# Value products one slot later, and one score product for both heads in narrow slots, in a fused attention and expert layer on one core

## The chip, the core and the metric

The kernel runs on one core of a Trainium2 chip. The metric is the device time in microseconds of one launch. TensorE does matrix products, VectorE and ScalarE read its result banks (PSUM), GpSimd works on SBUF only, and SyncE issues most transfers. Each engine works through its own list of instructions in order and waits on semaphores that the others raise.

## The reference

Batch 8, length 1024, width 256, 16 heads of 64, latent width 64, 32 experts:

```python
q = einsum('bld,dhk->blhk', x, Wq)
latent = einsum('bld,dc->blc', x, Wkv_down)
k = einsum('blc,chk->blhk', latent, Wk_up);  v = einsum('blc,chk->blhk', latent, Wv_up)
attn = softmax(where(causal, q k^T / sqrt(64), -inf))
x1 = layernorm(x + einsum('bqhd,hdo->bqo', attn v, Wout))
top1 = argmax(softmax(x1 @ w_router));  slot = expert's place if its place < capacity (320)
y = (silu(buf @ w_gate) * (buf @ w_up)) @ w_down        # per expert, on the gathered rows
out = layernorm(x1 + gate * y at the accepted tokens)
```

## The kernel before, in words

Wk_up is folded into the query weights and Wv_up into the output weights, so scores and value products are taken against the latent itself. The 16 heads are 8 pairs, the 8 batches give 64 pairs (`gp`; `b, p = divmod(gp, NPAIR)`). A pair is worked off in 12 slots (`SLOT`, line 48): slots 0 to 3 are the first 512 queries against key tiles 0 to 3, slots 4 to 11 the second 512 queries against key tiles 0 to 7. A tile on the diagonal needs only the queries from its own on, so slots 1, 2, 3 and 9, 10, 11 are 384, 256 and 128 queries wide for each head; slots 2, 3, 10 and 11 are the narrow ones.

For slot n (counted over all pairs), `turned_scores` (line 648) makes the scores with keys on the partitions, for each head two products: the high part of the latent (L660), then its low part with the row of negated maxima (L663). They go to `turned_ps[n % 2]`, a bank for each head. `exponentials` on ScalarE (L904) writes them into one of six buffers `probs`. `keep_past` on GpSimd (L440) zeroes the upper triangle of diagonal tiles, `add_probs` (L455 to L464) adds the buffer into the row sums. `values` on TensorE (L676) multiplies two slots' probabilities with the latent keys, both heads into `value_ps` (L683).

The maxima come from a second set of score products, `row_scores` (L636): two units in every slot, for the next pair, into the two banks `row_ps`. VectorE reduces each unit in turn (`row_max`, L1056 for diagonal units, L1060 for others), and unit n may start only once unit n - 2 is reduced. `turn_max` (L646) transposes eight columns of maxima, VectorE copies them (L1071) and SyncE puts them into `q_max` (L342 and L345).

All other products share one bank, `misc_ps`, in an order fixed by the tables `EARLY` and `LATE` (lines 240 to 280): in slot t of pair gp, TensorE does the scores, the `EARLY` uses, two units of row scores, the values, then the `LATE` uses. These are queries of the next pairs (`q`, L584), transposed maxima (`maxT`), row totals (`sums`, L693, turned and inverted by VectorE, L1077 to L1089), the output projection of the batch before (`proj`, L702, eight of them), its transposes (`x1T`, L720), router logits (L728) and counts of the places (`pos`, L736 to L741), and for the next batch the transposes of x (`xT`, L594), latents and keys. Each use waits until the reader of the one before has freed the bank. The other engines follow the same tables. Around them stand, at fixed pairs and slots, the steps of the layer norm and the routing: `variance` and `normalise` on VectorE, `roots` on GpSimd (L478 to L490), `choose` (from L1144) and `place` (from L1162) on VectorE, `gate_exponentials` on ScalarE, and GpSimd's `send` of rows to their experts' slots (L497), in pairs 4 and 5.

Before, the values of slots t - 2 and t - 1 come in every even slot t:

```python
if t % 2 == 0 and gp + t:
    values(gp * NSLOT + t - 2)
```

After the 64 pairs come `ENDING` (the last batch's rest) and then the 32 experts, which the change leaves as they are.

## Time and profile before

| | |
|---|---|
| time, median of 3 runs | 2686.41 us (2686.27 to 2687.94) |
| the profiled execution's own time | 2683.09 us |
| its span, first to last instruction | 2681.3 us |
| granted TensorE clock, mean | 0.972 of full speed |
| TensorE products busy | 2494.3 us (93%) |
| TensorE weight loads busy (beside products) | 1588.2 us |
| VectorE busy | 1550.2 us (58%) |
| ScalarE busy | 1002.2 us (37%) |
| GpSimd busy | 1701.7 us (63%) |

The spans are of one execution. PE is TensorE's product side, PEld its weight loads, DVE VectorE, ACT ScalarE, POOL GpSimd. A busy time is the union of its instructions' spans; matmuls overlap, and their ends are modelled. In a timeline, a row that merges several instructions gives the start of the first and the time to the end of the last; in brackets stands the idle time ahead of it and what ended it.

### The profile page before, as it was taken

Reading aid. Unit: us, or ns where it says so; the run is one execution under the profiler, and the core shown is the slowest. Engines: PE = TensorE matmul, PEld = TensorE weight load, DVE = VectorE, ACT = ScalarE, POOL = GpSimd, SP = SyncE. Lnnn points to the kernel's source line nnn. Section 1 sums busy time; section 2 is a strip of 40 time slices with the busy share of each in tenths; the row PEclk is TensorE's granted clock in tenths of the full one; section 3 lists DMA queues with packets and bytes.
Section 4 is the critical chain, followed back from the end, with each engine's and each line's share of the span. In section 5 each row is a group of like instructions: output and inputs, shape, how many; then the busy total and the mean of one; then the engine's idle time right before and its main releaser. Section 6 shows DMA issues by size and latency. Waiting matters only on the chain.

```text
span 2681.3 us, 35897 instructions
## 1 busy us (share of the span) xinstructions
PE 2494.3 (93%) x12072; PEld 1588.2 (59%) x12072; DVE 1550.2 (58%) x4378; ACT 1002.2 (37%) x1496; POOL 1701.7 (63%) x1671
## 2 busy tenths in 40 slices
PE   6999999999999999999999999999999999869996
PEld 4555665556655665566556655566556655646663
DVE  4566556665666566655665566656665665235553
ACT  3344334442444334433444244424443344112222
POOL 1677656865687658766786568656876578414444
PEclk7999999999999999999999999999999999879998
DMA  2121100200020001100110002000200011135441
GB/s 81 56 80 56 37 13 13 68 17 13 17 63 18 13 13 41 43 13 17 27 53 17 9 17 67 17 13 17 60 21 13 13 40 43 44 105 161 153 155 57
DMA packets 97062, 118.91 MB, mean 44 GB/s; under 512 B 12480, under 2 KB 75976, under 8 KB 96880
## 3 DMA queue, kind: packets, MB, share of 16 engines
q1 hardware_dynamic: 89712, 99.98, 13.3%
q0 software_dynamic: 7168, 16.64, 1.7%
q8 instruction: 98, 1.61, 0.2%
q14 instruction: 84, 0.69, 0.1%
HBM read 46.91 MB, written 37.90 MB: 32 GB/s over the span
## 4 chain that ended last, share of the span: by engine, by line
PE 63%; POOL 17%; issue 11%; DVE 5%; ACT 2%; DMA 0%; POOLq 0%; SPq 0%; ACTq 0%; DVEq 0%
PE value_ps L683 14%; POOL sums L464 10%; PE turned_ps L660 8%; PE row_ps L636 7%; PE turned_ps L663 7%; PE misc_ps L584 6%; PE turned_ps L844 5%; PE misc_ps L702 4%; PE misc_ps L693 4%; POOL probs L440 2%; PE value_ps L857 2%; PE misc_ps L857 2%; ACT probs L904 1%; POOL slots_x L497 1%; DVE masked_row L1056 1%
## 5 line engine op out<-in xcount | busy, mean ns | idle before, releaser
L904 ACT ACTIVATE probs<-turned_ps 128x1024 f32<-128x1024 f32 (+3 forms) x768 | 616.8, 811 | 959.6 <-PE turned_ps L663 951.3
L464 POOL TENSOR_TENSOR sums<-sums,probs 128x1024 f32<-128x1024 f32 (+3 forms) x512 | 830.2, 1622 | 23.2 <-ACT probs L904 14.2
L1056 DVE CUSTOM_DVE_ANT_0 masked_row<-row_ps,future 128x384 bf16<-128x384 f32 (+3 forms) x1024 | 464.2, 488 | 407.4 <-PE row_ps L636 406.2
L683 PE MATMUL value_ps<-probs,lat_keys 128*64 128x512 f32 (+3 forms) x3072 | 607.2, 507 | 44.7 <-POOL probs L440 41.3
L660 PE MATMUL turned_ps<-q_hl,lat_hi 128*128 128x512 f32 (+3 forms) x1536 | 569.6, 379 | 1.5 <-ACT fold_v L950 1.5
L663 PE MATMUL turned_ps<-q_max,lat_lo 65*128 65x512 f32 (+3 forms) x1536 | 528.0, 352 | 2.6 <-DMA q_max<-max_rows 2.6
L440 POOL TENSOR_SCALAR_AFFINE_SELECT probs<-probs 128x256 f32<-128x256 f32 x512 | 209.9, 410 | 498.1 <-ACT probs L904 497.4
L636 PE MATMUL row_ps<-lat_hi,q_hl 128*128 128x512 f32 (+3 forms) x1536 | 451.2, 365 | 14.2 <-DVE unit_max L1056 7.6
L460 POOL TENSOR_TENSOR sums<-probs 128x768 f32<-128x768 f32 (+1 forms) x128 | 268.6, 2098 | 229.9 <-ACT probs L904 229.9
L660 PEld LDWEIGHTS turned_ps<-q_hl,lat_hi 128*128 128x128 f32 x1536 | 293.8, 191 | 196.2 <-issue 148.3
L683 PEld LDWEIGHTS value_ps<-probs,lat_keys 128*64 128x64 f32 x3072 | 180.8, 137 | 348.8 <-issue 219.6
L1060 DVE TENSOR_REDUCE unit_max<-row_ps 128x1 f32<-128x512 f32 x512 | 327.7, 681 | 41.5 <-PE row_ps L636 36.7
L636 PEld LDWEIGHTS row_ps<-lat_hi,q_hl 128*128 128x128 f32 x1536 | 276.8, 192 | 90.2 <-DVE unit_max L1056 45.5
L663 PEld LDWEIGHTS turned_ps<-q_max,lat_lo 65*128 65x128 f32 x1536 | 295.0, 192 | 30.5 <-DMA q_max<-max_rows 2.9
L702 PE MATMUL misc_ps<-fold_v,headsT 128*128 128x256 f32 x1008 | 233.4, 385 | 2.4 <-POOL headsT L472 2.3
L702 PEld LDWEIGHTS misc_ps<-fold_v,headsT 128*128 128x128 f32 x1008 | 190.7, 193 | 34.9 <-issue 8.7
L1077 DVE STREAM_TRANSPOSE sums_cols<-misc_ps 128x512 f32<-128x512 f32 x127 | 91.0, 717 | 147.4 <-PE misc_ps L693 147.4
L472 POOL TENSOR_TENSOR headsT<-headsT,rinv_rows 128x512 f32<-128x512 f32 x128 | 164.0, 1282 | 1.9 <-DVE rinv_rows L1089 1.9
L886 ACT CAST q_hl<-misc_ps 64x512 fp32r<-64x512 f32 x125 | 72.6, 581 | 234.4 <-PE misc_ps L584 234.4
L844 PE MATMUL turned_ps<-ex_xT,ex_w 128*128 128x320 f32 x512 | 148.8, 445 | 0.0
L693 PE MATMUL misc_ps<-sums,ones_f 128*64 128x512 f32 x508 | 131.3, 595 | 7.7 <-DVE max_rows L1071 7.2
L1113 DVE TENSOR_TENSOR x<-misc_ps,x_in 128x256 f32<-128x256 f32 x64 | 27.2, 425 | 165.7 <-PE misc_ps L702 165.7
(183 smaller groups left out, 2408.7 us busy)
## 6 DMA issues: line engine op xcount, KB each, us to landing
q_max<-q_hl SPq DMA_DIRECT2D x256, 128.0 KB
slots_x<-zero_rows SPq DMA_DIRECT2D x8, 1290.0 KB, 6.2
ex_x<-slots_x SPq DMA_DIRECT2D x64, 129.0 KB, 3.5
x_in<-in_L_attn_x_bld SPq DMA_DIRECT2D x8, 1024.0 KB, 6.4
layer_out<-x_in SPq DMA_DIRECT2D x8, 1024.0 KB, 4.8
ex_w<-in_L_ffn_w_gate SPq DMA_DIRECT2D x32, 256.0 KB, 2.8
ex_w<-in_L_ffn_w_up SPq DMA_DIRECT2D x32, 256.0 KB, 3.2
ex_w<-in_L_ffn_w_down SPq DMA_DIRECT2D x32, 256.0 KB, 3.8
```

The costliest lines, as they stand in the source:

```text
L440: nc.gpsimd.affine_select(out=block, in_=block, pattern=[[0, 2], [1, P]], compare_op=ALU.is_ge, fill=0.0, base=0, channel_multiplier=-1).t ...
L460: nc.gpsimd.tensor_tensor(sums[c][:, :, q0:BANK], before[:, :, q0:BANK], now[:, :, q0:BANK], ALU.add).then_inc(added, 1)
L464: nc.gpsimd.tensor_tensor(sums[c][:, :, q0:BANK], sums[c][:, :, q0:BANK], now[:, :, q0:BANK], ALU.add).then_inc(added, 1)
L636: nc.tensor.matmul(dst[:, 0:k1 - k0], q_hl[gp % 2][:, h, i * P:(i + 1) * P], lat_hi[b % 2][:, k0:k1], start=True, stop=True).then_inc(rows ...
L660: nc.tensor.matmul(dst, lat_hi[b % 2][:, keys], q_hl[gp % 2][:, h, cols], start=True, stop=False)
L663: mm = nc.tensor.matmul(dst, lat_lo[b % 2][:, keys], q_max[:, c, h, q0:BANK], start=False, stop=True)
L683: mm = nc.tensor.matmul(value_ps[h * LD:(h + 1) * LD, q0:BANK], lat_keys[b % 2][:, j, :], probs[:, n % NPROBS, h, q0:BANK], start=(j == 0) ...
L702: mm = nc.tensor.matmul(bank[:, 0:D], headsT[:, (NPAIR * b + j) % NHEADS, i * P:(i + 1) * P], fold_v[:, j, :], start=(j == 0), stop=(j == ...
L844: mm = nc.tensor.matmul(turned_ps[f][:, m, 0:C], ex_w[e % AHEAD][:, m, kd, f * P:(f + 1) * P], ex_xT[:, e % 4, kd, :], start=(kd == 0), st ...
L904: nc.scalar.activation(probs[:, n % NPROBS, :, q0:BANK], turned_ps[n % 2][:, :, q0:BANK], ACT.Exp).then_inc(exp_done, 1)
L1056: nc.vector.tensor_tensor_reduce(masked_row[n % 2][:, 0:width], row_ps[n % 2][:, 0:width], future[:, BANK - width:], scale=-1.0, scalar=-M ...
L1060: nc.vector.tensor_reduce(dst, row_ps[n % 2][:, 0:width], AX.X, ALU.max, negate=True).then_inc(max_done, 1)
```

## The change

Four things are changed together. The value products of two slots are issued in odd slots t, for slots t - 3 and t - 2 (`LAG` = 1); what follows from them (the totals, the copies of `value_ps` on ScalarE, the second division on GpSimd, the keys) moves one slot as well. In the narrow slots the scores of both heads lie side by side in one bank, made by two products instead of four, and one exponential reads them. The shared bank's other uses are laid on other slots: four projections in each of pairs 0 and 1, all transposes in pair 2, logits and counts in pair 3. With them move `variance`, `normalise`, `roots` and `gate_exponentials`. In the last pair the projections move by one slot.

```diff
+    VALUES = 2
+    LAG = 1
@@ the tables of uses of the shared bank
             if gp:
-                late[4].append(("sums", gp - 1, 1))
-            late[6].append(("sums", gp, 0))
+                late[4 + LAG].append(("sums", gp - 1, 1))
+            late[6 + LAG].append(("sums", gp, 0))
-            if b and p == 0:
-                for i, t in enumerate((3, 5, 7, 10, 11)):
-                    late[t].append(("proj", b - 1, i))
-            if b and p == 1:
-                for i, t in enumerate((3, 5, 7)):
-                    late[t].append(("proj", b - 1, 5 + i))
-                for kd in range(KD):
-                    late[10 + kd].append(("x1T", b - 1, 0, kd))
+            if b and p in (0, 1):
+                for i, t in enumerate((3, 6, 10, 11)):
+                    late[t].append(("proj", b - 1, p * HPB + i))
             if b and p == 2:
-                for kd in range(KD):
-                    late[3 + 2 * kd].append(("x1T", b - 1, 1, kd))
-                late[7].append(("logits", b - 1))
+                for t, (hf, kd) in zip((3, 6, 10, 11), [(hf, kd) for hf in range(2) for kd in range(KD)]):
+                    late[t].append(("x1T", b - 1, hf, kd))
             if b and p == 3:
-                late[3].append(("pos", b - 1))
+                late[3].append(("logits", b - 1))
+                late[10].append(("pos", b - 1))
             if b + 1 < B and p == NPAIR - 2:
-                for t, c in zip((3, 5, 7, 8), (0, 2, 1, 3)):
+                for t, c in zip((3, 4, 6, 8), (0, 2, 1, 3)):
...
-                late[5].append(("keys", b + 1))
+                late[5 + LAG].append(("keys", b + 1))
...
-        for t, i in zip((1, 2, 3, 5, 7, 8, 9, 10), range(NT)):
+        for t, i in zip((2, 3, 4, 6, 8, 9, 10, 11), range(NT)):
+        in_one_bank = lambda t: 2 * (BANK - first_query(t)) <= BANK
+        def scores_of(n):
+            q0 = first_query(n % NSLOT)
+            if in_one_bank(n % NSLOT):
+                return turned_ps[n % 2][:, 0, 0:2 * (BANK - q0)].rearrange("p (h q) -> p h q", h=2)
+            return turned_ps[n % 2][:, :, q0:BANK]
@@ GpSimd
-                    if gp and t == 6:
+                    if gp and t == 6 + LAG:
                         divide(gp - 1, 1)
-                    if b and (p, t) in ((1, 0), (2, 0)):
+                    if b and (p, t) in ((1, 0), (2, 2 * LAG)):
                         roots(b - 1, p - 1)
@@ TensorE, turned_scores
+                if in_one_bank(t):
+                    nc.tensor.matmul(scores_of(n), lat_hi[b % 2][:, keys], q_hl[gp % 2][:, :, cols], start=True, stop=False)
+                    nc.tensor.matmul(scores_of(n), lat_lo[b % 2][:, keys], q_max[:, c, :, q0:BANK], start=False, stop=True
+                                     ).then_inc(turned_full, 1)
+                    return
@@ TensorE, the order in a slot
-                    if t % 2 == 0 and gp + t:
-                        values(gp * NSLOT + t - 2)
+                    if t % VALUES == LAG and gp * NSLOT + t >= VALUES:
+                        values(gp * NSLOT + t - LAG - VALUES)
@@ ScalarE
-                    if t == 0 and gp:
+                    if t == LAG and gp:
                         copy_heads(gp - 1, 1)
-                    if t == 4:
+                    if t == 4 + LAG:
                         copy_heads(gp, 0)
-                    if b and (p, t) == (2, 10):
+                    if b and (p, t) == (3, 6):
                         gate_exponentials(b - 1)
@@ VectorE
-                    if b and (p, t) in ((0, 11), (1, 8)):
+                    if b and (p, t) in ((0, 11), (1, 11)):
                         variance(b - 1, p)
-                    if b and (p, t) in ((1, 3), (2, 2)):
+                    if b and (p, t) in ((1, 3), (2, 5)):
                         normalise(b - 1, p - 1)
```

## Rows read from the trace of the kernel before

**Rows 1.** The page, part 1: busy time and share of the span by engine.
```profile
PE 2494.3 (93%) x12072; PEld 1588.2 (59%) x12072; DVE 1550.2 (58%) x4378; ACT 1002.2 (37%) x1496; POOL 1701.7 (63%) x1671
```
**Rows 2.** The waits of TensorE's products: total us, times, longest.
```profile
PE value_ps L683 <- POOL probs L440: 41.3, 42, 2.1
```
**Rows 3.** The windows: stretch and its length, busy by engine; plain pair, then batch 3.
```profile
125.35:154.83 29.48, 28.89 (x143) 17.19 (x142) 18.89 (x54) 13.12 (x19) 22.74 (x22) 1.00 0.22 63
884.53:930.46 45.93, 45.69 (x224) 32.22 (x222) 23.48 (x66) 13.18 (x19) 26.25 (x25) 1.00 0.08 18
930.46:972.10 41.64, 39.96 (x200) 27.10 (x199) 24.90 (x71) 13.57 (x19) 22.67 (x24) 1.00 0.03 7
972.10:1008.82 36.72, 34.63 (x186) 22.38 (x185) 23.18 (x65) 15.01 (x22) 25.01 (x26) 0.95 0.07 15
1008.82:1040.26 31.44, 29.76 (x152) 17.61 (x151) 21.77 (x67) 16.11 (x27) 22.89 (x22) 1.00 0.08 18
1040.26:1071.35 31.09, 29.37 (x144) 17.01 (x143) 18.93 (x54) 13.13 (x19) 27.00 (x26) 1.00 0.23 69
1071.35:1102.40 31.05, 29.33 (x144) 17.00 (x142) 18.89 (x54) 13.11 (x19) 26.87 (x26) 1.00 0.24 69
1102.40:1138.99 36.59, 33.35 (x172) 20.79 (x170) 23.49 (x63) 16.38 (x25) 26.34 (x25) 1.00 0.10 23
1138.99:1168.65 29.66, 29.31 (x151) 17.90 (x150) 18.70 (x51) 13.95 (x20) 19.29 (x18) 1.00 0.04 10
```
**Rows 4.** The timeline of TensorE's products in the plain pair: start us, us, line.
```profile
126.68 0.33 PE L636 MATMUL row_ps<-lat_hi,q_hl 128*128 128x128 f32 x1 [0.18 <-DVE unit_max L1056]
126.94 1.16 PE L683 MATMUL value_ps<-probs,lat_keys 128*64 128x256 f32 x8
128.03 0.27 PE L646 MATMUL misc_ps<-ident,neg_max 128*8 128x128 f32 x1
...
130.48 0.28 PE L660 MATMUL turned_ps<-q_hl,lat_hi 128*128 128x256 f32 x1
130.84 0.28 PE L663 MATMUL turned_ps<-q_max,lat_lo 65*128 65x256 f32 x1
...
133.22 0.28 PE L663 MATMUL turned_ps<-q_max,lat_lo 65*128 65x128 f32 x1
133.45 0.28 PE L663 MATMUL turned_ps<-q_max,lat_lo 65*128 65x128 f32 x1
...
134.53 0.40 PE L660 MATMUL turned_ps<-q_hl,lat_hi 128*128 128x512 f32 x1
134.77 0.40 PE L663 MATMUL turned_ps<-q_max,lat_lo 65*128 65x512 f32 x1
135.50 0.27 PE L646 MATMUL misc_ps<-ident,neg_max 128*8 128x128 f32 x1 [0.34 <-DVE neg_max L1056]
...
136.26 0.87 PE L683 MATMUL value_ps<-probs,lat_keys 128*64 128x256 f32 x8
136.96 1.03 PE L693 MATMUL misc_ps<-sums,ones_f 128*64 128x512 f32 x4
...
150.26 0.51 PE L636 MATMUL row_ps<-lat_hi,q_hl 128*128 128x384 f32 x2
...
152.16 1.72 PE L683 MATMUL value_ps<-probs,lat_keys 128*64 128x512 f32 x8
```
**Rows 5.** The same timeline, values of slots 0 and 1, pair 1 of batch 3.
```profile
936.00 1.08 PE L683 MATMUL value_ps<-probs,lat_keys 128*64 128x512 f32 x4
938.67 0.87 PE L683 MATMUL value_ps<-probs,lat_keys 128*64 128x384 f32 x4 [1.59 <-POOL probs L440]
```
**Rows 6.** The timeline of VectorE: first instruction of placing, and the one behind its last.
```profile
1018.72 0.42 DVE L1162 TENSOR_REDUCE rt<-work_b 128x8 f32<-128x256 f32 x1
...
1021.99 0.27 DVE L1071 CAST max_rows<-misc_ps 8x128 fp32r<-8x128 f32 x1
```
**Rows 7.** The variance's last step on VectorE: ns least, median, most; first and last start.
```profile
L1128 DVE TENSOR_SCALAR var_eps<-mean_var x16: 169/170/2034, 356.9 to 2334.2; 128x4 f32<-128x4 f32 x16
```

More of the change, by code:

```diff
@@ L240, in build_layer @@
         EARLY, LATE = {}, {}
+        last_sums = ("sums", PAIRS - 1, 1)
         for gp in range(PAIRS):
@@ L276, in build_layer @@
         LAST = B - 1
-        for t, i in zip((1, 2, 3, 5, 7, 8, 9, 10), range(NT)):
+        for t, i in zip((2, 3, 4, 6, 8, 9, 10, 11), range(NT)):
             LATE[PAIRS - 1, t].append(("proj", LAST, i))
-        ENDING = ([("sums", PAIRS - 1, 1)] + [("rest", LAST, i) for i in range(NT)]
+        ENDING = ([last_sums] + [("rest", LAST, i) for i in range(NT)]
                   + [("x1T", LAST, hf, kd) for hf in range(2) for kd in range(KD)] + [("logits", LAST), ("pos", LAST)])
@@ L666, in values @@
             def values(n0):
-                for n in (n0, n0 + 1):
+                for n in range(n0, n0 + VALUES):
                     gp, t = divmod(n, NSLOT)
@@ L677, in values @@
                     if n == n0:
-                        pe.wait_ge(exp_done, n0 + 2)
+                        pe.wait_ge(exp_done, n0 + VALUES)
                     if on_diagonal(t):
@@ L809, in _ @@
                         row_scores(*unit)
-                    if t % 2 == 0 and gp + t:
-                        values(gp * NSLOT + t - 2)
+                    if t % VALUES == LAG and gp * NSLOT + t >= VALUES:
+                        values(gp * NSLOT + t - LAG - VALUES)
                     for use in LATE[gp, t]:
                         STAGES[use[0]](*use[1:])
-            values(PAIRS * NSLOT - 2)
+            values(PAIRS * NSLOT - VALUES)
             for use in ENDING:
@@ L901, in exponentials @@
                     before = n - NPROBS
-                    act.wait_ge(values_done, before // 2 + 1)
+                    act.wait_ge(values_done, before // VALUES + 1)
                     act.wait_ge(added, before // NSLOT * NADD + ADDS_OF[before % NSLOT])
-                nc.scalar.activation(probs[:, n % NPROBS, :, q0:BANK], turned_ps[n % 2][:, :, q0:BANK], ACT.Exp
-                                     ).then_inc(exp_done, 1)
+                nc.scalar.activation(probs[:, n % NPROBS, :, q0:BANK], scores_of(n), ACT.Exp).then_inc(exp_done, 1)
             def copy_heads(gp, c):
@@ L911, in copy_heads @@
                 last = gp * NSLOT + (HPB - 1 if c == 0 else NSLOT - 1)
-                act.wait_ge(values_done, last // 2 + 1)
+                act.wait_ge(values_done, last // VALUES + 1)
                 nc.scalar.copy(headsT[:, gp % NHEADS, c * BANK:(c + 1) * BANK], value_ps[:, :]).then_inc(value_free, 1)
```

## The prediction

> **What bounds the kernel now.** I read the page first. TensorE is busy 2494.3 of 2681.3 us [rows 1], and it works in one fixed order, so the time is the length of its list plus the places where it stands still. Next the waits: for value products that found the triangle of GpSimd's mask not yet cut, the matmul side stood idle 41.3 us in 42 places [rows 2]. Then the length of each head pair: one plain pair of batch 0 (29.48 us) and the eight pairs of batch 3 (45.93, 41.64, 36.72, 31.44, 31.09, 31.05, 36.59, 29.66, together 284.12) [rows 3]. Last, the order of work inside a plain pair [rows 4]. A busy row there is not its cost, because matmuls overlap; the distance from one start to the next is.
>
> In the plain pair four waits can be read, all caused by another engine:
> - Slot 0: the second row-score product starts at 126.68, 0.18 us after an idle gap, and the values follow only at 126.94; with the two 128-wide products' 0.17 us the values could start 0.5 us sooner. VectorE has two row banks and reduces one unit at a time.
> - Slot 0: the values of slots 10 and 11 take 128.03 - 126.94 = 1.09 us; the same widths in slot 4 take 136.96 - 136.26 = 0.70. The 0.39 is GpSimd's cut.
> - Slot 4: the transposed maxima start at 135.50, behind an idle 0.34 us; from the last product (134.77) 0.73 us pass where 0.23 to 0.36 would do. About 0.4, VectorE again.
> - Slots 9 to 10: from the row scores of slot 9 (150.26) to the values (152.16) 1.90 us, for products that fill 0.35 + 0.48 + 0.56 = 1.39. 0.5 us, VectorE.
> Together 1.8 of 29.48 [rows 4]. So only 0.4 of a plain pair is the wait that a later value product cures; 1.4 belongs to VectorE's row maxima.
>
> Other pairs wait more for GpSimd. In pair 1 of batch 3 the values of slot 0 start at 936.00 and are through after 1.08 us, but those of slot 1 start only at 938.67, behind an idle 1.59 us, because GpSimd's roots stand ahead of the cut of slot 1 [rows 5]; against overlapping starts that is 1.8 us lost. Pair 2 (36.72) has such roots too, and pairs 4 and 5 are some 1.6 longer than the plain pair with no extra products: GpSimd's sends.
>
> **Part one, values a slot later.** The products are the same in number. Each cut and exponential gets the rest of a slot more. That is about 1 us for slots 10 and 11 (four 384-wide score products and two row scores, between 0.12 and 0.235 each [rows 4]), 2 us for slots 0 and 1 (two narrow slots with their row scores), over 1 us for slots 2 and 3. I take the plain pair's 0.4 us, pair 1's 1.8 in slot 2, the like in pair 2 (about 2.4) and pairs 4 and 5's 1.5 each as gone. What is late next is VectorE. Values have so far stood between row scores of slots 2 and 3, and of 10 and 11; now slot 2's row scores are followed at once by the narrow products and slot 3's row scores. This is just the pattern of slots 9 to 10, where 1.90 us pass from one row block to the values. For slot 3 that gives 1.91 against 0.45 + 0.24 + 0.52 = 1.2 without a wait: +0.70. For slots 10 to 11 the units are 512 wide, not 384, so I add 0.1: +0.8. Slots 5 and 7 lose their cover (values and totals now stand behind, not ahead of, their row scores): +0.35 and +0.15, estimates from the queue of maxima left by slots 4 and 6. One more change between kinds of product costs 0.1. Two waits of today (slot 0 and slots 9 to 10, 1.0) and the one in slot 4 (0.4) go, since the values now stand before them. Longer hold of the six probability buffers: the exponential six slots on still finds its value products three slots behind it; ScalarE's copies move with the values; no cost, and if that cover were gone ScalarE, busy 13 of 29 us [rows 3], would wait at once.
>
> **Part two, one product for both heads.** In the four narrow slots of a pair, four products become two of twice the width. From starts: three 256-wide starts from 130.48 to 130.84, 0.12 us each; two 128-wide starts from 133.22 to 133.45, 0.115 each; 512-wide from 134.53 to 134.77, 0.235 [rows 4]. So a 256-wide slot goes from 0.48 to 0.47: nothing. A 128-wide slot goes from 0.45 to 0.24, plus the slower first product behind values: 0.2 to 0.26 saved, twice a pair, 0.45 in all. No product here has a moving operand in two strides; below, it costs as one of its width; above, twice that (+0.24 and +0.47 a slot). I take the first, as every form above costs by its columns. But slots 3 and 11 are exactly those whose row scores now wait for VectorE, so this gain is mostly given back; it is inside the 1.2 above, and the 0.45 in the sum below stands against it.
>
> Plain pair: 29.48 - 1.8 - 0.45 + 0.7 + 0.8 + 0.35 + 0.15 + 0.1 = 29.3.
>
> **Part three, shared bank uses.** Batch 3 again, each pair as 29.3 plus its extra products. A projection is (45.93 - 29.48) / 5 = 3.3 us [rows 3]; a transpose 0.4, logits 3.5, counts 0.55, the next batch's transposes and latents 4.4 and its keys 0.65 are estimates, and their sizes cancel, since these products are only moved. Pair 0: four projections instead of five ( the one in slot 10 hides the 0.8 of slot 11): 41.8 (now 45.93). Pair 1: four projections, less that 0.8; the variance after slot 11 now stands before the next maxima, +0.35: 42.1 (41.64). Pair 2: four transposes, no logits, the same 0.35, half of slot 11's wait hidden, the normalisation in slot 5 costs slot 7 some 0.65: 31.4 (36.72). Pair 3: logits 3.5, counts 0.55, and expert choice (about 3 us on VectorE) now has no values beside it, +1.7: 35.0 (31.44). Pair 4: the placing chain, 1018.72 to 1021.99 = 3.3 us [rows 6], now stands before slot 11's maxima and the next pair's first row scores: +1.6 by VectorE's queue. Part of that chain can be held up by GpSimd: the variance's last step, 4 columns, takes 169 ns at its best, 2034 at its worst [rows 7]; GpSimd adds are dense in slots 10 and 11. I put 1.3 there (bounds 0 and 1.9 twice). Pair 4: 32.2 (31.09). Pair 5: 29.3 (31.05). Pair 6: its 4.4; waits for the single bank and its readers as today, 1.1; the latents in slot 10 lose the values that hid ScalarE's and VectorE's reading of the q bank, 2.6, and hide slot 11's 0.8: 36.6 (36.59). Pair 7: keys 0.65, which hide slot 7's wait; the maxima in slot 0 wait for the latents' bank, +0.85: 30.5 (29.66). Sum 278.9: -5.2 a batch.
>
> The Trainium skill's page "SBUF — State Buffer", section "SBUF: two separate sides", says that VectorE and GpSimd share a port pair that one holds for a whole instruction. The trace agrees: one instruction of 4 columns takes 0.17 or 2.03 us [rows 7]. Without that rule the batch would be 1.3 us shorter, 8 us over the kernel; with it hitting every step of the placing chain, 3 us longer.
>
> **The sum.** Batches 1 to 6: 6 x -5.2 = -31. Batch 0: five plain pairs -0.2 each, pair 7 +0.85: 0. Last batch without transposes and latents, with an end that GpSimd's adds hold: -6. Profiled execution 2683.1 (span 2681.3 and 1.8 around it) - 37 = 2646. The median shown is 3.3 above the profiled execution, hence 2649; I say 2648.
>
> **The rivals.**
> - B, the row maxima do not bite more than today. For it: they are a chain of only 0.6 us steps, and VectorE is busy 18.9 of 29.48 us [rows 3]. Against: slots 9 to 10 show the price in every pair. It gives back 2.1 - 1.4 = 0.7 us in some 64 pairs: 2648 - 45 = 2603.
> - C, the other side: VectorE's queue becomes the bound. Choice, placing, variance and normalisation now run where only 0.24 us of scores stand between two row blocks. It decides when the new VectorE waits exceed those of today by 1.3 us a pair (I have 0.7 in a plain one); at 1.5 us more than I count in half the pairs it gives 2648 + 48 = 2696.
> - D, GpSimd's cut is late again one slot on. For: in pairs 4 and 5 GpSimd is busy 27.00 and 26.87 of 31 us [rows 3], and its list is unchanged. Against: it idles in slots 5 and 6. Pairs 1, 2, 4 and 5 keep half their waits: 3.6 x 7 = +25, and the plain ones 0.2 x 40 = +8: 2681.
> - E, the wide product does not do what it says and costs double: +0.7 to 1.4 a pair, of which VectorE's waits hide about half: +35, 2683.
>
> **How the numbers follow.** Forecast 0.58 (own range 2625 to 2672), B 0.14, C 0.11, D 0.12, E 0.05. About 0.2% (5.4 us) is what a measurement can tell from no change. Faster by more than that (under 2681): 0.58 + 0.14 + half of D and a third of E + 0.02 = 0.81; within: 0.07; slower: 0.12. Range 2600 to 2684: it takes in B and most of D and E, and leaves C out.
>
> **What would show it.** Right: the waits of value products for GpSimd fall from 41.3 to under 10 us; plain pairs last about 29.3; from the row scores of slot 2 to the values of slot 3 come 1.9 us; row scores wait for VectorE in slots 3 and 11, not in 0 and 10; pairs 1 and 2 together lose about 5 us, while pair 3 grows by 3 to 4. Wrong: plain pairs under 28.6 (B) or over 30.2 (C); a 512-wide joined product spaced over 0.3 us (E); value products still idle on the mask in pairs 4 and 5 (D).

## The result: 2719 us, 1.2% slower

The changed kernel takes 2719.18 us (2717.53 to 2719.62 in four runs) against 2686.34 us of the kernel before (2684.18 to 2687.94, four runs): a ratio of 1.0117, interval 1.0101 to 1.0133. The forecast was 2648 us and faster. Its sign was wrong, and the time lies outside its range.

Page, part 1 of the kernel after, busy times by engine, to be held against [rows 1]:

```profile
PE 2508.9 (92%) x11560; PEld 1589.3 (59%) x11560; DVE 1562.7 (58%) x4378; ACT 1000.2 (37%) x1496; POOL 1704.3 (63%) x1671
```

There are 512 products fewer and no less TensorE time. The span is 2715.7 us, 34.4 more than before; the forecast had 37 fewer.

The waits of TensorE in the kernel after, total us, times, longest. L645 is the row-score product (L636 before), L1069 and L1073 are the maxima (L1056 and L1060 before).

```profile
PE row_ps L645 <- DVE unit_max L1073: 52.3, 103, 3.7
PE row_ps L645 <- DVE neg_max L1069: 21.5, 78, 2.8
PE misc_ps L593 <- DVE q_hl L1054: 18.7, 7, 2.7
...
PE row_ps L645 <- DVE unit_max L1069: 14.8, 16, 1.9
```

The row that headed this list before, 41.3 us of value products waiting for the mask [rows 2], is gone: the list has no wait of value products for GpSimd left. In its place stand 52.3 + 21.5 + 14.8 = 88.6 us in which the row scores wait for VectorE's maxima. In the kernel before the same three were small:

```profile
PE row_ps L636 <- DVE unit_max L1056: 7.6, 43, 0.2
...
PE row_ps L636 <- DVE neg_max L1056: 3.4, 3, 2.8
...
PE row_ps L636 <- DVE unit_max L1060: 2.4, 6, 0.6
```

One wait of the same kind became shorter: the transposed maxima, also made from what VectorE reduces, waited 9.8 us for it before and 0.9 after.

A longest wait of 3.7 us is what to follow: no maximum takes that long. The windows show in which pair it lies. These are the plain pair and the eight pairs of batch 3 in the kernel after, in the columns and the order of [rows 3]; the number behind the five busy times is the granted clock.

```profile
131.77:161.53 29.76, 28.76 (x137) 17.04 (x135) 18.86 (x53) 13.08 (x18) 22.83 (x22) 1.00 0.22 63
900.62:943.15 42.53, 41.97 (x201) 29.01 (x199) 20.86 (x58) 13.08 (x18) 24.14 (x23) 1.00 0.06 14
943.15:986.48 43.33, 42.38 (x200) 29.08 (x199) 23.54 (x70) 13.08 (x18) 25.45 (x26) 1.00 0.06 13
986.48:1024.43 37.95, 33.49 (x153) 19.38 (x151) 25.58 (x65) 14.62 (x21) 24.52 (x26) 0.91 0.06 15
1024.43:1059.45 35.02, 34.37 (x178) 22.06 (x176) 22.11 (x61) 16.99 (x28) 22.42 (x21) 0.95 0.07 16
1059.45:1093.39 33.94, 30.90 (x136) 18.02 (x134) 22.51 (x67) 13.12 (x18) 27.24 (x26) 0.95 0.21 63
1093.39:1123.20 29.81, 28.82 (x136) 17.07 (x134) 18.86 (x53) 13.08 (x18) 26.94 (x26) 1.00 0.27 72
1123.20:1159.72 36.52, 33.14 (x164) 20.71 (x163) 21.87 (x58) 16.11 (x24) 24.22 (x23) 1.00 0.07 15
1159.72:1190.89 31.17, 29.47 (x143) 17.50 (x141) 20.13 (x55) 14.07 (x20) 21.51 (x20) 1.00 0.08 18
```

| pair of batch 3 | before | forecast | after | off by |
|---|---|---|---|---|
| 0 | 45.93 | 41.8 | 42.53 | +0.7 |
| 1 | 41.64 | 42.1 | 43.33 | +1.2 |
| 2 | 36.72 | 31.4 | 37.95 | **+6.6** |
| 3 | 31.44 | 35.0 | 35.02 | 0.0 |
| 4 | 31.09 | 32.2 | 33.94 | **+1.7** |
| 5 | 31.05 | 29.3 | 29.81 | +0.5 |
| 6 | 36.59 | 36.6 | 36.52 | -0.1 |
| 7 | 29.66 | 30.5 | 31.17 | +0.7 |
| sum | 284.1 | 278.9 | 290.3 | +11.4 |

The whole difference of the spans: batches 1 to 6 took 25.9 us more, batch 0 8.4 (4.1 of it in its first pair, 48.57 against 44.46, where the granted clock is lower: 0.72, 0.61 and 0.93 in its three thirds, 0.79, 0.79 and 1.00 before), the start 2.0, the last batch's pairs 5.6 more, the ending 7.5 less; together 34.4.

Batch 3 was the shortest batch of the kernel before. There pair 2 took 36.7 us in three of the seven batches, 38.3 to 38.4 in three and 39.8 in one, with a granted clock from 0.95 down to 0.87, and batches 1 to 6 lasted 285.8 us on average, not 284.1. In the changed kernel pair 2 took 38.0 to 38.2 in all seven. So pair 2 didn't get longer on average (37.9 before, 38.0 after): the 5.3 us that the forecast took off it did not come, while pairs 1, 3, 4 and 7, with their new steps, grew by 1.5, 3.5, 2.8 and 1.5.

**Pair 2.** The timelines of GpSimd, VectorE and TensorE, slots 5 to 7 of pair 2, kernel after (start us, us, as in [rows 4]):

```profile
1001.47 2.39 POOL L469 TENSOR_TENSOR sums<-probs 128x1024 f32<-128x1024 f32 x1
1004.01 2.34 POOL L473 TENSOR_TENSOR sums<-sums,probs 128x1024 f32<-128x1024 f32 x1
...
1001.82 5.32 DVE L1146 TENSOR_SCALAR x<-x,mean_var,rstd 128x256 f32<-128x256 f32 x4
1007.06 1.28 DVE L1073 TENSOR_REDUCE unit_max<-row_ps 128x1 f32<-128x512 f32 x2
...
1003.73 0.40 PE L677 MATMUL turned_ps<-q_max,lat_lo 65*128 65x512 f32 x1
1007.80 1.18 PE L645 MATMUL row_ps<-lat_hi,q_hl 128*128 128x256 f32 x2 [3.67 <-DVE unit_max L1073]
```

Read it by the times of the ends. The four normalising instructions take 5.32 us. The last two of them run only when GpSimd's second add has ended (1006.35). In the kernel before, where the four stood in slot 2, they took 1.64, and GpSimd's next add started only 0.17 us before they ended:

```profile
979.97 1.64 DVE L1133 TENSOR_SCALAR x<-x,mean_var,rstd 128x256 f32<-128x256 f32 x4
...
981.44 1.86 POOL L460 TENSOR_TENSOR sums<-probs 128x768 f32<-128x768 f32 x1
```

In the changed kernel, behind the four in VectorE's list stand the maxima of slot 6, and TensorE, which needs their bank for the next row scores, does nothing for 3.67 us. The source lines of the normalisation, before and after (ns least, median, most), have the same median, 408, but a longest of 501 before and 2568 after. The same instruction takes six times as long in some places, so its place or its neighbour makes the difference; experiment 6 decides.

```profile
L1133 DVE TENSOR_SCALAR x<-x,mean_var,rstd x64: 395/408/501, 371.8 to 2336.5; 128x256 f32<-128x256 f32 x64
```

```profile
L1146 DVE TENSOR_SCALAR x<-x,mean_var,rstd x64: 397/408/2568, 376.2 to 2372.2; 128x256 f32<-128x256 f32 x64
```

The wait isn't all. Windows of the kernel after, the stretch of the stall and the one behind it, then the same two for the stall in pair 4:

```profile
1002.60:1007.80 5.20, 1.53 (x10) 1.00 (x8) 5.20 (x6) 2.24 (x3) 3.60 (x2) 0.86 0.00 0
1007.80:1013.70 5.90, 5.88 (x14) 1.81 (x14) 2.08 (x7) 0.00 (x0) 1.27 (x1) 0.55 0.01 3
1059.45:1063.00 3.55, 1.50 (x7) 0.86 (x5) 3.41 (x14) 1.02 (x1) 2.76 (x5) 1.00 0.02 5
1063.00:1068.30 5.30, 5.30 (x23) 3.89 (x24) 1.72 (x10) 1.40 (x2) 3.99 (x5) 0.68 0.16 54
```

In the 5.9 us after the first stall the granted clock is 0.55, so nearly all of them pass at the lower of the two levels, 1.2 GHz.

**Pair 4.** The placing chain meets an add of GpSimd too, in one step, which took 0.24 us before:

```profile
1059.72 1.27 POOL L473 TENSOR_TENSOR sums<-sums,probs 128x512 f32<-128x512 f32 x1
...
1059.85 1.17 DVE L1191 SCALAR_TENSOR_TENSOR rt<-rt 128x8 f32<-128x8 f32 x1
...
1062.48 0.30 PE L645 MATMUL row_ps<-lat_hi,q_hl 128*128 128x128 f32 x1 [1.83 <-DVE unit_max L1069]
```

TensorE waits 1.83 us for the maxima behind the chain, and the clock then is 0.68 in 5.3 us.

### The profile page after: what moved, and what is told of

The parts are those of the page before. It is cut to its first block, busy times and chain, and to the rows that moved or that the text cites. A ratio compares the mean times of both kernels' runs of the same rounds, so it can differ in the third digit from the quotient of the medians.

```text
span 2715.7 us, 34873 instructions
## 1 busy us (share of the span) xinstructions
PE 2508.9 (92%) x11560; PEld 1589.3 (59%) x11560; DVE 1562.7 (58%) x4378; ACT 1000.2 (37%) x1496; POOL 1704.3 (63%) x1671
## 4 chain that ended last, share of the span: by engine, by line
PE 79%; DVE 14%; issue 4%; POOL 2%; ACT 1%; DMA 0%; POOLq 0%; DVEq 0%; SPq 0%; ACTq 0%
PE value_ps L697 20%; PE row_ps L645 10%; PE misc_ps L716 8%; PE misc_ps L593 8%; PE turned_ps L674 7%; DVE unit_max L1073 6%; PE turned_ps L677 5%; PE turned_ps L858 5%; PE misc_ps L707 4%; PE value_ps L871 2%; PE misc_ps L871 2%; PE turned_ps L668 2%; DVE x L1146 1%; PE row_ps L847 1%; PE turned_ps L669 1%
## 5 line engine op out<-in xcount | busy, mean ns | idle before, releaser
L1069 DVE CUSTOM_DVE_ANT_0 masked_row<-row_ps,future 128x384 bf16<-128x384 f32 (+3 forms) x1024 | 464.9, 486 | 282.6 <-PE row_ps L645 275.3
L697 PE MATMUL value_ps<-probs,lat_keys 128*64 128x512 f32 (+3 forms) x3072 | 599.3, 512 | 0.0
L645 PE MATMUL row_ps<-lat_hi,q_hl 128*128 128x512 f32 (+3 forms) x1536 | 486.4, 377 | 95.8 <-DVE unit_max L1073 52.3
L674 PE MATMUL turned_ps<-q_hl,lat_hi 128*128 128x512 f32 (+1 forms) x1024 | 435.6, 425 | 1.7 <-ACT fold_v L963 1.7
L645 PEld LDWEIGHTS row_ps<-lat_hi,q_hl 128*128 128x128 f32 x1536 | 287.9, 193 | 237.2 <-DVE unit_max L1073 110.8
L1073 DVE TENSOR_REDUCE unit_max<-row_ps 128x1 f32<-128x512 f32 x512 | 329.6, 685 | 137.8 <-PE row_ps L645 137.7
L677 PE MATMUL turned_ps<-q_max,lat_lo 65*128 65x512 f32 (+1 forms) x1024 | 396.1, 387 | 1.8 <-DMA q_max<-max_rows 1.8
L697 PEld LDWEIGHTS value_ps<-probs,lat_keys 128*64 128x64 f32 x3072 | 190.7, 139 | 244.1 <-issue 200.6
L674 PEld LDWEIGHTS turned_ps<-q_hl,lat_hi 128*128 128x128 f32 x1024 | 196.4, 192 | 171.3 <-issue 138.8
L716 PEld LDWEIGHTS misc_ps<-fold_v,headsT 128*128 128x128 f32 x1008 | 188.6, 190 | 46.6 <-issue 20.5
L677 PEld LDWEIGHTS turned_ps<-q_max,lat_lo 65*128 65x128 f32 x1024 | 198.1, 193 | 27.6 <-DMA q_max<-max_rows 2.3
```

The source lines that it names most:

```text
L645: nc.tensor.matmul(dst[:, 0:k1 - k0], q_hl[gp % 2][:, h, i * P:(i + 1) * P], lat_hi[b % 2][:, k0:k1], start=True, stop=True).then_inc(rows ...
L674: nc.tensor.matmul(dst, lat_hi[b % 2][:, keys], q_hl[gp % 2][:, h, cols], start=True, stop=False)
L677: mm = nc.tensor.matmul(dst, lat_lo[b % 2][:, keys], q_max[:, c, h, q0:BANK], start=False, stop=True)
L697: mm = nc.tensor.matmul(value_ps[h * LD:(h + 1) * LD, q0:BANK], lat_keys[b % 2][:, j, :], probs[:, n % NPROBS, h, q0:BANK], start=(j == 0) ...
L716: mm = nc.tensor.matmul(bank[:, 0:D], headsT[:, (NPAIR * b + j) % NHEADS, i * P:(i + 1) * P], fold_v[:, j, :], start=(j == 0), stop=(j == ...
L1069: nc.vector.tensor_tensor_reduce(masked_row[n % 2][:, 0:width], row_ps[n % 2][:, 0:width], future[:, BANK - width:], scale=-1.0, scalar=-M ...
```

## The experiments

**Theory 1:** two moved VectorE chains, the normalisation above all, are held up by GpSimd's adds, TensorE waits behind them, and its clock falls. **Theory 2:** the loss is in every pair. The values stood as cover between row scores and their maxima, and the one-slot lag takes this cover away wherever something is added. Each ratio is to the kernel before in the same session (medians 2689.03 for runs 1 to 4, 2689.88 for 5 to 8, and 2688.01 for 9 to 12).

### 1. Normalise earlier (2716.12 us, ratio 1.010, 1.0083 to 1.0117)

```diff
-                    if b and (p, t) in ((1, 0), (2, 2 * LAG)):
+                    if b and (p, t) in ((1, 0), (2, 0)):
                         roots(b - 1, p - 1)
-                    if b and (p, t) in ((1, 3), (2, 5)):
+                    if b and (p, t) in ((1, 3), (2, 2)):
                         normalise(b - 1, p - 1)
```

> The changed kernel (2719.2 us) with two steps put back: GpSimd's roots of the second half at the head of pair 2 (slot 0 instead of 2), VectorE's normalisation of that half in slot 2 instead of slot 5. Theory 1 (a shared lock and the clock): in pair 2 the four normalising instructions last 5.32 us beside GpSimd's adds of slots 5 and 6, TensorE's row scores of slot 7 wait 3.67 us, and the granted clock then falls to half for 6.8 us, which costs another 2.3. Taken away, pair 2 goes from 37.9 to about 32.5 us, seven times: 2719 - 38 = 2681 (2675 to 2692). Theory 2 (lost cover in every pair): VectorE's row maxima cost in every pair and pair 2 only moves its wait: 2708 to 2719.

Missed: 3 us gained by the medians, not 38, and the two intervals overlap. The same timeline, pair 2 of this kernel:

```profile
989.83 3.92 DVE L1146 TENSOR_SCALAR x<-x,mean_var,rstd 128x256 f32<-128x256 f32 x4
990.00 1.91 POOL L469 TENSOR_TENSOR sums<-probs 128x768 f32<-128x768 f32 x1
...
995.24 0.27 PE L655 MATMUL misc_ps<-ident,neg_max 128*8 128x128 f32 x1 [3.15 <-DVE neg_max L1069]
```

The instructions now met the adds of slots 1 and 2: 3.92 us, and 3.15 us of TensorE. Pair 2 took 36.17 (forecast table: 31.4), pair 3 36.59 instead of 35.02. "Slot 2" was no safe place; in the kernel before it was one because GpSimd's add came later (981.44, as the chain ended). So this run couldn't decide between the theories, but it made theory 1 sharper: what counts would be which adds run, and not the slot's number.

### 2. Values ahead of the row scores (2715.57 us, 1.0094, 1.0076 to 1.0113)

```diff
+                    if t % VALUES == LAG and gp * NSLOT + t >= VALUES:
+                        values(gp * NSLOT + t - LAG - VALUES)
                     for unit in UNITS_AT.get((gp, t), []):
...
-                    if t % VALUES == LAG and gp * NSLOT + t >= VALUES:
-                        values(gp * NSLOT + t - LAG - VALUES)
```

> The changed kernel with one order turned: in odd slots the value products stand ahead of the two row-score products instead of behind them. Theory 2 (lost cover): the values again part the row scores of slots 2 and 3 (1.91 us from row scores to values now, of which 0.7 is a wait), 4 and 5, 6 and 7, 10 and 11 (0.9 waited). A plain pair goes from 29.8 to 28.9 or less, and pair 2's wait of 3.67 us is half hidden by 1.77 us of values: 2719 - 58 - 14 = 2647 (2630 to 2665). Theory 1 (only the lock and the clock): plain pairs change by less than 0.3, pair 2 gains 2: 2690 to 2712. Theory 3 (GpSimd's cut is late again, since the values come 0.2 to 1 us sooner): waits for L449 come back, over 20 us of them, 2690 or more.

Missed, and with it theory 2 as the main cause: the values again cover VectorE's maxima in each odd slot, yet plain pairs came to 29.67 only (29.76), and pairs 0 and 1 grew to 43.70 and 44.95. Value products wait for GpSimd again, 12.6 us. Pair 2 fell from 37.95 to 34.61, so the values hide part of the stall; the time still lies outside theory 1's range too (2690 to 2712).

### 3. No lag, the new spread kept (2757.22 us, 1.0251, 1.0234 to 1.0268)

```diff
-    LAG = 1
+    LAG = 0
```

> The changed kernel with LAG = 0: values in even slots for slots t - 2 and t - 1, totals, copies, second division and keys back by one slot, roots of the second half at the head of pair 2; joined narrow products and the new spread of the shared bank stay. If the lag itself is the loss (theory 2), plain pairs go from 29.8 to 29.2 or less (the joined products' 0.2 to 0.4 off the 29.48 of the kernel before) and the waits for GpSimd's cut come back (30 us or more): 2675 to 2695. If the new spread is the loss (theory 1: normalisation in slot 5, placing in slot 10), it stays within 10 us of 2719.

Missed, far on a side that neither theory had: within the new spread the lag is no part of the loss, it is worth 38 us there. Plain pair and pair 2's normalisation, kernel without lag:

```profile
127.53:156.81 29.28, 28.65 (x136) 16.38 (x135) 18.92 (x54) 13.12 (x18) 22.77 (x22) 1.00 0.22 64
```

```profile
1008.98 2.37 POOL L469 TENSOR_TENSOR sums<-probs 128x1024 f32<-128x1024 f32 x1 [2.90 <-ACT probs L918]
...
1009.23 6.21 DVE L1146 TENSOR_SCALAR x<-x,mean_var,rstd 128x256 f32<-128x256 f32 x4
...
1012.58 2.39 POOL L473 TENSOR_TENSOR sums<-sums,probs 128x1024 f32<-128x1024 f32 x1
...
1017.32 0.90 PE L734 MATMUL misc_ps<-ident,x 128*128 128x128 f32 x3 [5.14 <-DVE sums_cols L1090]
```

In a plain pair the lag costs half a microsecond (29.28 against 29.76). But the batch takes 296.7 us instead of 290.3: pair 2 39.80, pair 4 36.80, with a normalisation of 6.21 us and a TensorE wait of 5.14. Waits of value products for GpSimd are back to 39.5 us. Without the lag the totals share slot 6 with a projection or transpose, so this run undoes more than the lag alone.

### 4. Four products in narrow slots again (2722.28 us, 1.0117, 1.0101 to 1.0134)

```diff
-        in_one_bank = lambda t: 2 * (BANK - first_query(t)) <= BANK
+        in_one_bank = lambda t: False
```

> The changed kernel with four products in the narrow slots again, one for each head and part, in two banks. My forecast's step: the joined product saves 0.2 us in each 128-wide slot, but its row scores wait for VectorE right behind it, so nothing comes of it: within 7 us of 2719 (2716 to 2730). Rival: the saving of 0.45 us a pair counts in full: 2719 + 29 = 2748. Second rival: the joined product has slowed the kernel: 2700 or less.

No difference, a plain pair of 29.77. Under the lag the joined product is worth nothing; VectorE's maxima take back what it saves.

### 5. Normalise on ScalarE (2674.48 us, 0.9941, 0.992 to 0.9961)

```diff
@@ VectorE, variance
+                if b < LAST:
+                    nc.vector.tensor_scalar(less_mean[:, tiles], mean_var[:, tiles, 0], -1.0, None, ALU.mult)
@@ GpSimd, roots
+                if b < LAST:
+                    nc.gpsimd.tensor_tensor(act_bias[:, tiles], less_mean[:, tiles], rstd[:, tiles], ALU.mult)
@@ ScalarE
+                for i in range(hf * HPB, (hf + 1) * HPB):
+                    nc.scalar.activation(x1[:, i, 0:D], x1[:, i, 0:D], ACT.Identity, bias=act_bias[:, i:i + 1],
+                                         scale=rstd[:, i:i + 1])
@@ VectorE, batches 0 to 6
-                        normalise(b - 1, p - 1)
```

> The changed kernel (2719.2 us) with both mid-kernel normalisations done by ScalarE (4 activations of 256 columns, 0.5 us each, with a bias that GpSimd and VectorE prepare in two tiny steps) at the same slots, (1, 3) and (2, 5). The four VectorE instructions last 1.37 us where no add of GpSimd runs beside them (first half), 5.3 in slot 5, 3.9 in slot 2 (run e1), 6.2 with lag 0 (run e3). Theory 1, sharpened (VectorE's normalising instruction is locked out while GpSimd's add runs, which stalls TensorE 3.7 us and lets its clock fall): pair 2 goes from 37.9 to 32 us or less, the half-clock stretch at its slot 7 is gone: 2719 - 41 = 2678 (2670 to 2688). Theory 2 (VectorE's queue is too long there by its own work): 1.37 us come off that queue, pair 2 gains 1.5 to 2: 2705 to 2710.

As expected, and the deciding run: (x - mean) / deviation as x * scale + bias on an engine that isn't VectorE takes 44.7 us off the changed kernel (by the medians), and turns slower into faster. Windows of pairs 2 and 4:

```profile
976.03:1007.38 31.35, 30.54 (x153) 18.73 (x151) 20.45 (x62) 16.37 (x25) 24.69 (x27) 1.00 0.08 18
...
1042.40:1076.33 33.93, 30.87 (x136) 18.09 (x134) 22.50 (x67) 13.12 (x18) 27.13 (x26) 0.95 0.21 63
```

Pair 2 has the length that was forecast for it (31.4) and a granted clock of 1.00, and pair 4 is as it was. The two profiled executions differ by less, 2715.7 to 2677.6, 38.1 us: pair 2 gains 46.6 in its seven batches and pair 1 some 4, but pair 3 took 36.5 to 36.6 in five of the seven (35.0 after) and pair 6 38.1 to 39.2 in three of six (36.5 after).

Run 5 still isn't the forecast's kernel, 26 us above 2648. And it is no faster than run 7 below, from the same session, which has the joined products alone (2671.9): in this form the lag and the new spread bring nothing beyond those, even with the normalisation off VectorE. Of the kernels that leave nothing out, only runs 8 and 10 get below them.

### 6. The adds taken away instead (2688.12 us, 0.999, 0.998 to 1.0001)

Left out: GpSimd's additions to the row sums for slots 5 and 6 of pair 2.

```diff
@@ GpSimd, add_probs, slot 6; slot 5 likewise
+                    if gp >= NPAIR and gp % NPAIR == 2 and t == 6:
+                        nc.gpsimd.tensor_copy(ident8[:, :], ident8[:, :]).then_inc(added, 1)
+                        return
```

> The changed kernel, GpSimd's two adds into the row sums of slots 5 and 6 left out in pair 2 of batches 1 to 7 (a two-column copy keeps the semaphores; these row sums lack two key tiles). VectorE's list is untouched. Theory 1 (locked out by the add): the four normalising instructions go from 5.3 us to 1.4, pair 2 from 37.9 to 32 us, the clock does not fall there: 2678 to 2688. Theory 2 (VectorE's own queue): they stay at 5.3 us and the time at 2715 or more.

```profile
992.42 1.34 DVE L1154 TENSOR_SCALAR x<-x,mean_var,rstd 128x256 f32<-128x256 f32 x4
```

VectorE's list is that of the changed kernel, its place is the same, only the adds beside it are missing: 1.34 us instead of 5.32, and pair 2 at 31.72. So it is the adds that hold it up. Pair 2 gains 6.2 to 6.4 us in each of seven batches, 44 in all, but the kernel only 31: pair 6 took 38.05 to 39.29 in six of these batches (36.5 after), and pair 3 about 36.5 in four of the seven (35.0 after). What sets the clock in those pairs when pair 2 gets shorter wasn't tested.

### 7. The kernel before, with joined products only (2671.9 us, 0.9932, 0.9912 to 0.9952)

> The kernel before (2686 to 2689 us) with the joined narrow products alone. In run e3 (lag 0, joined) a plain pair lasts 29.27 us against 29.48: 0.2 a pair of the 0.45 that the products save, since the maxima wait the rest: 2687 - 13 = 2674 (2670 to 2680), pairs with waits for GpSimd's cut gain less. Rival: nothing, as in the changed kernel (run e4 within 4 us of it): 2684 or more.

Right. The edit is the part of the change with `in_one_bank` and `scores_of`; nothing is moved.

```profile
130.04:159.38 29.34, 28.70 (x136) 16.36 (x134) 18.96 (x54) 13.14 (x18) 22.79 (x22) 1.00 0.22 64
```

```profile
PE value_ps L697 <- POOL probs L449: 57.4, 84, 2.1
```

Without the lag and the new spread the joined product does gain, 18 us in all by the medians and 0.14 in the plain pair, although its values then wait longer for the mask (57.4 us against 41.3).

### 8. Run 5, and the counts of places in slot 6 of pair 3 (2666.14 us, 0.9912, 0.989 to 0.9933)

```diff
             if b and p == 3:
                 late[3].append(("logits", b - 1))
-                late[10].append(("pos", b - 1))
+                late[6].append(("pos", b - 1))
```

> Run e5 and the counts moved from slot 10 of pair 3 to slot 6. In the changed kernel the placing chain stands before slot 11's maxima; one of its steps takes 1.17 us instead of 0.24 beside an add, the row scores of pair 4's slot 0 wait 1.8 us and the clock falls for 3.4 us, so pair 4 lasts 33.9 us against 29.8 for pair 5. In slot 6 the values, totals and scores of slots 7 and 8 cover it. Theory 1: pair 4 falls to 30 to 31, pair 3 stays within 1 of 35: another 20 to 25 us below e5, 2655 (2648 to 2665). Rival: the chain's 3.3 us come back in pair 3's slots 7 and 8 (pair 3 grows by over 2): within 8 us of e5.

Half right. Windows of pairs 3 and 4:

```profile
1000.60:1039.13 38.53, 36.57 (x178) 22.45 (x176) 25.48 (x73) 17.12 (x28) 22.40 (x21) 0.91 0.07 15
1039.13:1068.89 29.76, 28.77 (x137) 17.05 (x135) 18.86 (x53) 13.10 (x18) 26.98 (x26) 1.00 0.24 72
```

Pair 4 loses the whole 4.2 us that the placing chain had cost it (33.93 to 29.76), with the clock at 1.00. Pair 3, which now holds choice, counts and placing, takes 3.5 more in this batch and drops to 0.91; over the seven batches its mean goes from 36.1 in run 5 to 38.1. In batches 1, 3, 4 and 6 its length in run 5 is 36.5, 35.0, 36.5, 35.1, so it already varied with the same work. 8 us were gained.

### 9. The kernel before with my best spread (2678.81 us, 0.9966, 0.9952 to 0.998)

No lag, joined products, ScalarE's normalisation (slot 8 of pair 1, slot 7 of pair 2), the gate's exponentials in slot 5 of pair 3, projections as before, and:

```diff
             if b and p == 2:
-                    late[3 + 2 * kd].append(("x1T", b - 1, 1, kd))
-                late[7].append(("logits", b - 1))
+                    late[10 + kd].append(("x1T", b - 1, 1, kd))
             if b and p == 3:
-                late[3].append(("pos", b - 1))
+                late[3].append(("logits", b - 1))
+                late[5].append(("pos", b - 1))
@@ GpSimd
-                    if b and (p, t) in ((1, 0), (2, 0)):
+                    if b and (p, t) in ((1, 5), (2, 5)):
                         roots(b - 1, p - 1)
```

> The kernel before with joined narrow products (run e7, 2672 us), both normalisations on ScalarE (slots (1, 8) and (2, 7)), GpSimd's roots moved from slot 0 of pairs 1 and 2 to slot 5, where GpSimd idles 3 us, the second half's transposes in slots 10 and 11 of pair 2, logits in slot 3 and counts in slot 5 of pair 3. No lag. If the waits for GpSimd's cut can be cured by moving the roots instead of the values: pair 1 from 41.4 to 39.6 us, pair 2 from 36.5 to 30.5, pair 3 from 31.4 to 35.5, together 3.5 to 4 a batch: 2646 (2638 to 2655). Rival: roots in slot 5 make the second half's cuts and adds late: 2665 or more.

Missed by 33 us, and slower than run 7, on which it is built (0.9932). Windows of pairs 1, 2 and 3:

```profile
926.76:967.90 41.14, 39.43 (x193) 26.33 (x191) 24.12 (x69) 15.65 (x23) 22.58 (x25) 1.00 0.03 8
967.90:997.51 29.61, 29.28 (x145) 17.09 (x144) 18.91 (x54) 16.04 (x24) 25.93 (x28) 1.00 0.09 19
997.51:1035.66 38.15, 34.66 (x179) 21.10 (x177) 26.79 (x74) 17.19 (x28) 22.13 (x21) 0.96 0.07 15
```

Pair 2 came out at a plain pair's length, but pair 3, which now holds choice, counts and placing and in which VectorE is busy 26.8 us, took 38.15, about as in run 8 (38.53); in three other batches it took 40.1 to 41.6. Pair 1 gained half a microsecond of its 41.64 here, and took 42.5 to 42.7 in three other batches. Which of pair 3's steps costs how much wasn't separated.

### 10. Run 8, and the latents' first two uses apart (2654.12 us, 0.9872, 0.9856 to 0.9889)

```diff
-                late[10].append(("lat", b + 1, 0))
-                late[11].append(("lat", b + 1, 1))
+                late[11].append(("lat", b + 1, 0))
             if b + 1 < B and p == NPAIR - 1:
+                late[0].append(("lat", b + 1, 1))
```

> Run e8 (2666 us) with the next batch's first latents in slot 11 of pair 6 instead of 10, the second in slot 0 of pair 7 instead of 11. In e8 the first latents, as the row scores ahead of them, take 3.3 us for 0.5 us of products in slot 10, since ScalarE and VectorE must first read the q bank and no values stand between. My forecast priced this at 2.6 for pair 6 and 0.85 for pair 7. With values between: pair 6 falls by 3 (1.5 us of it moves to pair 7), pair 7 rises by about 2: net 1 to 2 us in 7 batches: 2656 (2650 to 2663). Rival: the wait only moves, 2664 or more.

Right in the time, and the fastest kernel here that leaves nothing out: 1.3% faster than the kernel before, 2.4% faster than the changed one. The two pairs moved by more than expected: pair 6 fell by 4.8 us (38.28 to 33.45) where 3 was expected, and pair 7 rose by 4.2 (31.16 to 35.39; 3.0 in three of six batches) where 2 was. The 18.7 us in which the latents wait for VectorE's reading of the q bank (third row of the waits after) are gone from its list. Windows of pairs 6 and 7:

```profile
1095.51:1128.96 33.45, 32.33 (x159) 19.84 (x157) 21.27 (x57) 15.06 (x22) 24.18 (x23) 1.00 0.08 17
1128.96:1164.35 35.39, 32.70 (x150) 19.83 (x148) 20.72 (x56) 15.13 (x22) 21.61 (x21) 0.95 0.07 16
```

### 11 and 12. Short maxima, in the changed kernel and in the one before (2610.08 and 2668.95 us, one execution each)

Left out: VectorE's maxima read only 128 columns of each unit, the last of a diagonal unit and the first of any other. TensorE's work is the same.

> The changed kernel with VectorE reducing only 128 columns of every row-score unit (the maxima leave out keys; TensorE's list is untouched). It takes VectorE's row maxima out of the way. My forecast counted 2.0 us of waits for them in a plain pair of the changed kernel, of 29.3: the plain pair (29.77 now) falls to 27.7 to 28.0. Rival (the waits are not VectorE's): above 29.3.

> The same edit in the kernel before. Counted there: 1.4 us of waits for VectorE in a plain pair, 0.4 for GpSimd's cut. The plain pair (29.48) falls to 28.0 to 28.2; the difference of the two falls says what the lag cost in cover: 0.3 to 0.7 us a pair.

The plain pair of each:

```profile
117.94:145.65 27.71, 27.71 (x137) 17.10 (x135) 12.59 (x53) 13.06 (x18) 22.92 (x22) 1.00 0.23 67
```

```profile
120.53:149.44 28.91, 28.00 (x143) 17.10 (x142) 12.57 (x54) 13.13 (x19) 22.78 (x22) 1.00 0.22 65
```

```profile
PE value_ps L683 <- POOL probs L440: 83.9, 84, 2.2
```

In the changed kernel the maxima cost 29.76 - 27.71 = 2.05 us of a plain pair, and nothing else holds TensorE: it is busy 27.71 of 27.71. Run 11 is as expected. In the kernel before they cost 29.48 - 28.91 = 0.57, not the 1.3 or more expected, because the values then wait for GpSimd's mask instead, 83.9 us in all (the row is this run's). So the lag did remove its wait, and the place was taken by VectorE, by about the amount counted.

## Why the prediction was wrong

Point by point:

- **The waits it set out to remove.** Right: 41.3 us of value products waiting for GpSimd fell to none, and pair 5 lost 1.24 us of the 1.75 expected. Rival D is out. Run 3 shows what the wait would be in the new spread: 39.5 us.
- **What takes their place in a plain pair.** Right in kind, short by 0.45 of 29.3. The pattern after slot 2 came as forecast; timeline of the plain pair, kernel after:

```profile
136.89 0.51 PE L645 MATMUL row_ps<-lat_hi,q_hl 128*128 128x384 f32 x2
...
137.89 0.49 PE L645 MATMUL row_ps<-lat_hi,q_hl 128*128 128x512 f32 x1 [0.25 <-DVE neg_max L1069]
...
138.80 1.72 PE L697 MATMUL value_ps<-probs,lat_keys 128*64 128x512 f32 x8
```

  136.89 to 138.80 is 1.91 us, the forecast's 1.91. From row scores to values, slots 5 and 7 take 0.70 us each, and 0.27 and 0.34 in run 11: they wait 0.43 and 0.36 where 0.35 and 0.15 stood. Run 11 measures all of VectorE's waits at 2.05 where the terms add up to 2.0; B is out. So the missing 0.45 isn't in the new waits. Without them the pair lasts 27.71, and the forecast's other terms make 29.48 - 1.8 - 0.45 + 0.1 = 27.33: what the change was to save was put 0.4 too high. In 64 pairs that is about 25 us.
- **Joined products.** They cost by their columns as assumed: a 512-wide one (two heads of 256) is spaced 0.235 us from the next, like any other. E is out. What they save is hidden by VectorE in the changed kernel (run 4), while in the kernel before they gave 18 us (run 7).
- **The step that failed.** In part three, pair 2: "the normalisation in slot 5 costs slot 7 some 0.65". Pair 2 took 6.6 us more than its forecast: TensorE stood still for 3.67 us and then worked 5.9 us at a granted clock of 0.55. Seven batches make 46; run 5, which takes the normalisation off VectorE, brings pair 2 to its forecast (31.35), and run 6 does so nearly (31.72) with the engine unchanged and only the adds gone. The term of 0.65 weighed the chain by its position in VectorE's own list, where it lasted 1.64 us before. The adds beside its new place, which made it 5.32, are on GpSimd's list.

  The page "SBUF — State Buffer" of the Trainium skill (section "Who interferes with whom") says that a `tensor_scalar` can enter a mode that uses the port pair shared with GpSimd, and that whoever comes first blocks the other for the whole instruction. The traces agree: 5.32 us beside the adds, 1.34 without them. The prediction drew on the same rule, which [rows 7] had shown, but weighed it on the placing chain alone; it left out the longest run of `tensor_scalar` instructions that the change moves.
- **Placing in pair 4.** The lock was given 1.3 us, and hit one step by 0.93 (0.24 to 1.17). What came on top is again the wait behind it and the clock: 33.94 against 32.2. Run 8 puts the whole chain's cost there at 4.2 us.
- **The other sums of part three.** Pair 3 (35.0, 35.02), pair 6 (36.6, 36.52), pair 7 and pair 0 (0.7 too low, of which 0.45 is the plain pair's) held. Pair 1 was 1.2 too low; 0.5 of it goes with its own normalisation in run 5 (43.33 to 42.82).
- **Batch 0, the start and the last batch** were priced at 0 and -6 and came at +10.4 and -1.9. Its first pair's +4.1 was not taken apart.
- **The batch that stood for all.** "Batches 1 to 6: 6 x -5.2" starts from batch 3 of the kernel before, which was the shortest. The six batches lasted 1.7 us more on average, so the same forecast of 278.9 a batch would have meant -41 and not -31. The spans miss the forecast by 71 us: pair 2 of batches 1 to 6 makes 40, their other pairs 28, batch 0 and the start 10, the last batch and the ending 4, less 10 for this.
- **A slip in a sum.** Pair 7's terms, 29.3 + 0.65 - 0.15 + 0.85, make 30.65 and not 30.5.
- **The signs.** Of the signs of being right, one failed: pairs 1 and 2 together were to lose about 5 us and grew from 78.4 to 81.3. None of the signs of being wrong was met, and none looked at GpSimd's adds beside the normalisation.
- **The rivals.** C had the right engine and side, and 2696, but the wrong mechanism: it spread a queue over half the pairs. Two chains in two pairs of eight were enough. Its chance of 0.11 was too small for a change that moves chains of an engine which GpSimd can hold up [rows 7].

How much of pair 2's loss is wait and how much is clock isn't settled to the tenth. Over the loop from 300 to 2250 us the granted clock stood at its lower level for 95.6 us in the changed kernel and 68.3 in run 5, added up over its stretches. As work at half speed takes twice as long, these 27.3 us are about 13.7 lost; seven waits of 3.67 make 25.7. Together 39, against the 38.1 between the two profiled executions. This is an estimate: some 1.5 us of each stretch at the lower level lie inside the wait, so about 5 us are counted twice.

Not tried: the lag with the old spread of the shared bank, which would price the lag by itself. Of the parts of the change, only the joined products were tried alone; the lag and the new spread were not separated from each other in full.

## What to carry to other kernels

Before moving an instruction to another slot, look at what the neighbour engines do at the new time, not only at what stands ahead of it on its own list: of four VectorE instructions, two adds on GpSimd made 5.3 us out of 1.3. Price a stall of TensorE with what follows it; in these traces a wait of 3.7 us was followed by nearly 6 us at half clock. And where such a chain can run on another engine, try it there: ScalarE in run 5 alone turned 1.2% slower into 0.6% faster. And take the average of all batches as the starting point of a sum, not one batch: here the one chosen was 1.7 us shorter than the average.

## What the runs showed of the hardware

- Four `tensor_scalar` instructions of 128x256, fp32, SBUF to SBUF: 1.34 us undisturbed, 3.92, 5.32 and 6.21 us where they met GpSimd's adds. One by one, the four in pair 2 of the changed kernel took 2.19, 2.56, 0.40 and 0.40 us: the first ended 0.15 us after the first add, the second 0.15 us after the second, so the second add got in between two instructions of the chain. Even an instruction of 128x8 took 1.17 us beside an add instead of 0.24. GpSimd's masks and copy of 128x256 (0.44 to 0.55 us each) beside the same four cost them 0.3 us in all: 1.64 in the kernel before.
- The granted clock fell after a wait of 1.83 us in pair 4 too, and in runs 5 and 6 it stayed up or fell from one batch to the next in pairs 3 and 6, with the same list of work (35.0 or 36.5 us; 36.5, 38.1 or 39.3). In the kernel before pair 2 took 36.7, 38.4 or 39.8. In these kernels a pair's length isn't fixed by its own work to better than 1.5 to 3 us.
- Making one wait shorter can pay for another: with short maxima the plain pair of the kernel before gained 0.57 us, and over the whole kernel its values' waits for GpSimd doubled, from 41.3 to 83.9 us.
